# A decoder layer with 16 experts: row numbers read in pairs, and the output index moved behind the gated value

## The reference

```
x = x + shift_attention(layernorm(x))
x = x + cross_attention(layernorm(x), ctx, ctx)        # 16 heads, 77 keys
h = layernorm(x)
logits = h @ Wg.T + bg;  the 2 best experts of 16, softmax over the two gives cw
gu = h @ Wgu + bgu;  gate = min(gu[::2], 7);  up = clip(gu[1::2], -7, 7)
gated = (up + 1) * gate * sigmoid(1.702 * gate)
x = x + sum over the 2 experts of cw * (gated @ Wd + bd)
```

## Time and profile before

| | |
|---|---|
| time, median of 3 runs | 670.28 us (670.08 to 670.28) |
| profiled execution, span | 699.0 us |
| its time outside the span | the page gives none |
| TensorE, busy share of the span | 79% |
| VectorE, busy share | 69% |
| GpSimd, ScalarE | 49%, 47% |
| mean granted TensorE clock | 0.913 |

### The profile page before, as it was taken

The page is one execution under the profiler, slowest core; times in us unless marked ns, Lnnn a source line. Parts: engine busy times, 40 slices in busy tenths (PEclk is TensorE's granted clock), DMA queues, the critical chain, the costliest instruction groups (busy, mean ns, idle before and its releaser), DMA issues.

```text
span 699.0 us, 12908 instructions
## 1 busy us (share of the span) xinstructions
PE 551.6 (79%) x3216; PEld 294.1 (42%) x3217; DVE 479.4 (69%) x1334; ACT 328.5 (47%) x707; POOL 345.7 (49%) x455
## 2 busy tenths in 40 slices
PE   1896979778878788888879599978588999999910
PEld 0575534322434434334433245544244555555500
DVE  4577545857568685849675648868575777777796
ACT  3862753464687666656755133422232333333331
POOL 4757440442865866676774513445532333333353
PEclk9999988759999998979997779999999999999955
DMA  9912000039101010100010112355553333333398
GB/s 312 297 41 24 0 5 0 1 110 302 46 3 34 32 47 21 41 21 34 29 54 8 62 31 68 86 91 136 149 148 77 90 82 70 82 88 91 99 377 295
DMA packets 93415, 62.61 MB, mean 90 GB/s; under 512 B 68338, under 2 KB 78710, under 8 KB 93240
## 3 DMA queue, kind: packets, MB, share of 16 engines
q1 hardware_dynamic: 85352, 44.12, 23.5%
q0 software_dynamic: 6864, 16.86, 7.1%
q10 hardware_dynamic: 1152, 1.06, 0.5%
HBM read 27.97 MB, written 25.56 MB: 77 GB/s over the span
## 4 chain that ended last, share of the span: by engine, by line
PE 32%; DVE 21%; SPq 15%; issue 13%; ACT 8%; another core or an unknown queue 4%; DMA 4%; POOL 3%; ACTq 0%; DVEq 0%; POOLq 0%
SPq L416 8%; PE bank L1154 7%; PE bank L968 4%; SPq L417 3%; PE bank L1170 3%; SPq L412 3%; DVE AR L1559 2%; PE bank L957 2%; ACT AR L803 2%; DVE X L1880 2%; DVE MX L1547 2%; PE bank L995 2%; PE bank L1015 2%; DMA X<-in_x 2%
## 5 line engine op out<-in xcount | busy, mean ns | idle before, releaser
L665 POOL DMA_INDIRECT y_rows<-AR,CST x79 | 77.2, 977 | 152.3 <-ACT AR L903 142.1
L892 ACT ACTIVATE AR<-AR 128x256 f32<-128x256 f32 x79 | 32.9, 417 | 148.8 <-DVE AR L1788 120.1
L543 POOL TENSOR_TENSOR W<-STG,W 128x512 f16<-128x512 f32 (+1 forms) x48 | 55.5, 1162 | 55.5 <-ACT W L706 53.5
L622 POOL DMA_INDIRECT xs_rows<-AR,SLOT x64 | 63.3, 988 | 36.6 <-issue 19.5
L1559 DVE RECIPROCAL AR<-bank 128x512 f32<-128x512 f32 x16 | 53.7, 3355 | 25.7 <-PE bank L1154 25.3
L803 ACT ACTIVATE AR<-bank 104x1024 f32<-104x1024 f32 (+1 forms) x48 | 48.4, 1022 | 46.1 <-PE bank L1138 23.0
L1547 DVE TENSOR_REDUCE MX<-bank 128x8 f32<-128x616 f32 x64 | 48.5, 794 | 27.5 <-PE bank L1103 14.8
L1804 DVE TENSOR_TENSOR AR<-bank,AR 128x256 f16<-128x256 f32 x79 | 33.6, 425 | 34.8 <-ACT AR L896 31.8
L1788 DVE TENSOR_SCALAR AR<-bank 128x256 f32<-128x256 f32 x79 | 33.3, 422 | 29.9 <-PE bank L1295 24.3
L1154 PE MATMUL bank<-AR,VCUR 104*32 104x512 f32 (+1 forms) x256 | 40.9, 744 | 13.8 <-issue 10.0
L1302 PE MATMUL bank<-ID,AR 128*128 128x128 f32 x158 | 33.0, 291 | 21.6 <-DVE AR L1799 15.9
(11 more groups left out here) (249 smaller groups left out, 1413.9 us busy)
## 6 DMA issues: line engine op xcount, KB each, us to landing
W<-in_wexp SPq DMA_DIRECT2D x16, 768.0 KB, 5.6
W<-y_rows SPq DMA_DIRECT2D x8, 1024.0 KB, 14.7
X<-in_x SPq DMA_DIRECT2D x4, 1024.0 KB, 12.7
out<-X SPq DMA_DIRECT2D x8, 512.0 KB, 8.6
CST<-in_cst SPq DMA_DIRECT2D x1, 1309.0 KB, 9.1
CST<-xs_rows SPq DMA_DIRECT2D x79, 1.0 KB
y_rows<-AR,CST POOLq DMA_INDIRECT x79
xs_rows<-STG SPq DMA_DIRECT2D x9, 129.0 KB
```

Source lines behind the costliest of these rows:

```text
L543: pool.tensor_tensor(w[:, 1], STG[:, q], w[:, 0], ALU.subtract).then_inc(s["w_split"], 1)
L622: pool.indirect_dma_start(xs_rows, bass.IndirectOffsetOnAxis(ap=SLOT[:, par, k, j:j + 1], axis=0), RB[:, par, j, :], None, bounds_check=XS ...
L665: pool.indirect_dma_start(y_rows, bass.IndirectOffsetOnAxis(ap=NIX[:, k:k + 1], axis=0), CY[:, k, :], None, bounds_check=TOPK * NTOK - 1, ...
```

## The change

SyncE no longer reads a row number for each slot. VectorE makes a second table `ROW2` beside the others, one word for two slots: row number of the odd slot divided by 128, times 1024, plus that of the even slot divided by 128. SyncE reads one word for two slots (`row_pair`), takes it apart by remainder and quotient in registers, asserts the range of both parts and multiplies them by 128. The number of DMAs and their sizes stay. On VectorE, `copies` gets one instruction for the divided rows (`ROWF`) and one for `ROW2`, in each of its two calls. In the loops of slots 32 to 78, `c_index` moves from behind `c_gate` to behind `c_glu`.

```diff
+RADIX = 1024
+LASTROW = NEXP * CAP // P
...
+        ROWF = free(594 + 13 * NEXP, P)
+        ROW2 = free(594 + 13 * NEXP + P, P // 2, I32)
...
+        def row_pair(eng, t):
+            v = eng.value_load(ROW2[0:1, ds(t, 1)], min_val=0, max_val=LASTROW * (RADIX + 1))
+            return [nc.s_assert_within(r, 0, LASTROW) * P for r in (v % RADIX, v // RADIX)]
...
-            def load(n, q, first=False):
-                row = sp.value_load(TAB[0:1, ds(P + n, 1)], min_val=0, max_val=XS_ROWS - P)
+            def load(n, q, row, first=False):
...
             for n in range(EARLY):
-                load(n, n % IN, n < IN)
+                if n % 2 == 0:
+                    rows = row_pair(sp, n // 2)
+                load(n, n % IN, rows[n % 2], n < IN)
...
             with sp.Fori(EARLY // IN, NSLOT // IN) as t:
-                for q in range(IN):
-                    load(t * IN + q, q)
+                for q in range(0, IN, 2):
+                    rows = row_pair(sp, t * 2 + q // 2)
+                    load(t * IN + q, q, rows[0])
+                    load(t * IN + q + 1, q + 1, rows[1])
             for n in range(NSLOT // IN * IN, NSLOT):
-                load(n, n % IN)
+                if n % 2 == 0:
+                    rows = row_pair(sp, n // 2)
+                load(n, n % IN, rows[n % 2])
...
+                dve.tensor_scalar(ROWF[0:1, n0:n1], rows[:, P + n0:P + n1], 1.0 / P, None, ALU.mult)
                 dve.tensor_copy(PAIR[0:1, n0:n1], rows[:, n0:n1]).then_inc(s["quad_s"], 1)
                 dve.wait_ge(s["quad_s"], at + 1)
...
+                two = ROWF[0:1, :].rearrange("p (t v) -> p t v", v=2)
+                dve.scalar_tensor_tensor(out=ROW2[0:1, a0:a1], in0=two[:, a0:a1, 1], scalar=float(RADIX),
+                                         in1=two[:, a0:a1, 0], op0=ALU.mult, op1=ALU.add)
...
                 for k in range(IN):
                     c_gate(t * IN + k, k % 2)
-                    c_index(t * IN + k, k, t)
                     c_gl(t * IN + (k - 1), (k - 1) % 2)
                     c_glu(t * IN + k, k % 2)
+                    c_index(t * IN + k, k, t)
             for n in range(NSLOT // IN * IN, NSLOT):
                 c_gate(n, n % 2)
-                c_index(n, n % IN, n // IN)
                 c_gl(n - 1, (n - 1) % 2)
                 c_glu(n, n % 2)
+                c_index(n, n % IN, n // IN)
```

## The result

The changed kernel takes 668.18 us, median of 13 runs (663.08 to 672.4), and the kernel before 670.28 us, median of 13 (666.49 to 673.99). The ratio is 0.9952, 95% interval 0.9929 to 0.9975: faster by 0.5%, or 3.2 us by the ratio, where the two medians stand only 2.1 apart. My forecast was 664.3. Ratios and intervals in this document leave out executions more than 1.5% above the fastest of the same kernel; the medians include them.

The account below looks back on a forecast made before the run. SyncE's queue was taken to bound slots 32 to 78: 14.7 us saved less 8.7 for decoding, plus 0.3 from earlier slots, is 6.3, scaled to 6.0, from 670.28 to 664.3 us; range 660.2 to 671.5.

Parts of the forecast that it names:

- SyncE's queue is the bound: Slots 32 to 78: SyncE's pace of 2.87 us a slot sets the time, against TensorE's 2.69.
- the rule that the prediction sets against itself: Trainium skill: a small DMA costs mostly completion latency, some 2 us, not setup, so the issue's surroundings would hardly matter.
- The rival that it was hidden there: Expert stage in timed runs: SyncE's pace is 2.57, under TensorE's 2.69, so nothing is gained; 670.0 us, chance 0.21.
- the scaling by 0.959: Whole kernel: profile span of 699.0 us scaled evenly to the timed 670.28, making the 6.3 us gain 6.0.
- The odd slot's 0.64 us: SyncE, odd slots 33 to 77: each loses the whole row reading, 23 times 0.64, 14.7 us less.
- The decoding: SyncE, even slots 34 to 78: taking the word apart costs 0.38 us each, 8.7 us; ends 0.14 and 0.92.
- Slots before 32: SyncE from slot 28 on: 0.3 us less; earlier slots are set by VectorE's routing work and gain nothing.
- TensorE takes over: Rival, expert stage: decoding is cheap and the cap holds, 8.9 us less, 661.7 us; chance 0.14.
- the cap of 8.9: Load 78 waits for slot 74's products and index, so it can't start before 648.1: at most 8.9 us less.
- The index for nothing: VectorE, slots 32 to 78: moving the index behind the gated value costs zero, its round 2.44 us, under 2.69.

Follow-up runs that it names:

- read_twice: The kernel before, with SyncE reading each row number twice; 707.36 us (two runs), ratio 1.0526 to the kernel before.
- before2: The kernel before, unchanged, run and profiled a second time; ratio 1.0002, span 670.8 us.
- after_dve_adds: The changed kernel with all 64 last additions on VectorE, GpSimd's additions and ScalarE's scalings taken out; ratio 0.9859 to the kernel before.
- index_only: The kernel before with only the output index moved behind the gated value, SyncE still reading a row number per slot; ratio 0.9996.
- after2: The changed kernel, unchanged, run and profiled again; ratio 0.9919 to the kernel before, span 661.4 us.
- pair_only: The changed kernel with the output index put back behind the gate, keeping the reading in pairs; ratio 0.9994 to the kernel before.
- after_no_last: The changed kernel without GpSimd's scatter of the last slot, 78, which holds no rows; ratio 0.9922 to the kernel before.

## Why the prediction came out as it did

- **SyncE's queue is the bound: right.** read_twice shows it in timed runs: 37 us more, where by the rule that the prediction sets against itself the reading would hardly matter. The rival that it was hidden there is out, and with it the scaling by 0.959: that step took 28.7 us for the cost of profiling, when it was one unusual execution. It made 0.3 us of the forecast, and a fifth of the chances.
- **The odd slot's 0.64 us: close.** Odd distances fell by 0.57 us, from 2.76 and 2.69 in before2 to 2.20 and 2.11. Reading a second time cost 0.57 in read_twice as well.
- **The decoding: over-sized.** Between undisturbed rounds, 11.33 us in before2 and 10.55 now, it is 0.78 us, 0.39 a pair, so decoding costs 0.64 - 0.39 = 0.25 us, where I took 0.38. Most of the new register work is in two rows, of line 348 in the loop (count, ns min/median/max); each is once for a pair:

```profile
L348 SPq FUSED_REGOPS  x21: 102/104/104, 505.1 to 611.7; - x21
L348 SPq SEQ_ASSERT  x21: 18/18/18, 505.3 to 611.8; - x21
```

  One instruction of 104 ns and one assertion appear beside the ones that were there, instead of two and two. The rest is in the register instruction just before each odd slot's transposing load (L423, 103 to 113 ns, where those of even slots take 46 to 51).
- **Slots before 32: put at almost nothing.** I took 0.3 us less there, since VectorE's routing set them. The kernels that read pairs take 105.8 to 106.5 us for slots 0 to 32, those that read each number 107.5 to 108.5 (117.0 in the unusual first profile), so it was 1.0 to 2.7 us.
- **TensorE takes over: the rival was the better forecast.** With 0.39 a pair the sum on SyncE is 9.0 us less from slot 32 on; it was 8.9 against before2. SyncE waits 0.6 us in all for the index, so the cap of 8.9 held no load back. But TensorE no longer waits for rows behind slot 32, and its slots 33 to 74 start at 502.02 and 612.59, 2.70 us each. I had 2.69, where SyncE's round is now 2.64 a slot. My sum was made at SyncE's load of slot 78 and took for granted that TensorE follows it. It didn't: 2.8 of the 11.2 us by which this load is earlier stayed there. I had given TensorE 0.14 and should have given it most of the forecast's chance.

```profile
502.02 0.38 PE L1303 MATMUL bank<-BEX,CST 128*128 128x512 f16 x1
...
612.59 0.38 PE L1303 MATMUL bank<-BEX,CST 128*128 128x512 f16 x1
```

- **The index for nothing: right where it was priced.** Its round on VectorE stays under TensorE's: gate, gated value and index at 611.80, 613.77, 614.12, the next gate at 614.30, 2.50 us. At the last slot it had a use that I had not seen, 2.1 us in the profiles with all additions on VectorE, though the times don't show it clear of noise.
- **The end: the step that is missing.** The prediction let the time behind the last load stand as it was, 39 us from the issue of the result loads. It read that SyncE issues the result loads right behind it, and didn't ask what else would be under way then. In the kernel before, TensorE's slot 78 starts 0.4 us behind the issue of the result loads, and VectorE's additions stand a moment at the second group of results (at 640.35 in before2; read_twice has there 0.28 us of waiting for these loads), just before GpSimd's last scatter. In the changed kernel TensorE is the one behind: slot 78 starts at 624.02, 3.2 us behind the result loads (620.78), and when VectorE is free of the last slot, at 629.4, the results are there. Its additions then have no gap, and the scatter that comes 3.2 us into them has to wait. In the two profiles this costs 3.9 us.

So that the time fell inside my range is in part luck. The queue was the bound and reading in pairs shortened it, as forecast. But a gain on SyncE of 11.2 us, where I had 6.3, lost 2.8 to a TensorE that couldn't follow and 3.9 at an end that the forecast didn't have.

## What to carry to other kernels

When a stage is made faster, count the gain at the engine that comes second, and look at the first thing behind the stage that was ordered by the old lateness. An engine may get in where another one idles, and a speed-up can take those idle moments away. Reading two small numbers in one word pays on a queue that issues DMAs back to back (0.64 us for 0.25), and a second execution of the kernel before is worth having before its profile is scaled.

## What the runs showed of the hardware

Work of GpSimd can be held by VectorE over many instructions, not only over one. A scatter that takes 0.97 us was held 16.7 us over VectorE's additions in the changed kernel, 23.05 us in after_dve_adds, and 4.84 us where VectorE idled 0.16 us. Where both work, VectorE's group of four additions takes 2.13 us instead of 1.67, and GpSimd's addition 0.83 instead of 0.68 us (10.91 for sixteen alone). The Trainium skill (SBUF — State Buffer, section Who interferes with whom) says that the two engines share one pair of ports as an exclusive lock, held for a whole instruction, and that a VectorE instruction with two inputs in SBUF contends with a GpSimd instruction that reads SBUF. The trace agrees that they contend: the additions of both are slower together. For the scatter it shows more than the length of one instruction, a wait over 41 of VectorE's additions in the changed kernel.

For slot 78's scatter the profiles agree with each other. In before, before2, index_only and read_twice VectorE's second group starts 0.51 to 0.76 us behind the start of the addition before it, and the scatter begins 0.7 to 1.2 us behind that and takes about 1 us, beside running additions. In the changed kernel, after2, pair_only and the four profiles with all additions on VectorE the starts are 0.40 us apart up to the scatter and on, and it is held, in after2 until VectorE idles.

That a gap is always needed is not shown. In the changed kernel GpSimd's scatter of slot 77 began at 631.22, 1.8 us into the same unbroken additions, and took 1.11 us, and in after_no_last GpSimd's first addition got in 2.9 us into them. What makes the difference to slot 78's scatter, 3.2 us in, is open.
